# A transformer layer with routed experts: expert rows in units of 256 slots, outputs scattered back by row number

## The chip, the cores and the metric

The kernel runs on one core of a Trainium2 chip. The metric is the time of one launch on the device, in microseconds (us), as the median of several runs. The profile comes from one further execution, whose own time is given beside its span.

## The reference

One layer: a normalised input goes through causal attention with 16 heads and through a mixture of experts, and both are added to the input. 16 batches of 256 tokens give 4096 tokens of 128 numbers.

```python
xn = layernorm(x)
x  = x + attention(xn) + moe(xn)

def moe(x):                                   # 4096 tokens, H = 128, F = 512, E = 8, TOP_K = 2
    probs = softmax(x @ Wg)
    vals, idx = top_k(probs, 2)
    weights = vals / (sum(vals) + 1e-9)       # two weights for each token
    y = silu(x @ W1[e] + b1[e]) @ W2[e] + b2[e]        # for the token's two experts
    shared = silu(x @ Ws1 + bs1) @ Ws2 + bs2
    return sum_over_two(weights * y) + 0.1 * shared
```

## The kernel before

The first two thirds of the launch are attention: 64 groups of four heads run through a software pipeline whose beats `(t, s)` are written out in one loop for each engine. The router works beside it, on groups of 8 tiles (1024 tokens). For each token and each of its two experts it finds a place in a table of rows in HBM, `rows_d` (`expert_rows`), in which each expert has a region of its own. POOL writes the normalised rows there by indirect DMAs of 128 rows each (`scatter`, L851), one or two in a beat. Near the end of attention `list_blocks` on DVE turns the counts into a list of blocks: a block is 512 slots of one expert. SP fills the unused slots of an expert's last block with zeros (`fill`).

After attention come the passes (`PASSES`, `NP` = 31). A pass takes 512 tokens through two layers. A shared pass, of which there are 8 (two first, six last), reads its tokens in order from a store of split, turned rows. A routed pass (23, `NB`) loads the 512 rows of one block and the two weight matrices of its expert, both by a number read from the block list. 23 is the number that is enough for every possible distribution of 8192 rows over 8 experts in whole blocks of 512.

Each operand is in two parts (a high part and the rest), and each product takes three matmuls. In iteration `m` of the final loop PE issues: `turn_block(m+2)` (4 transposes, L1843), `hidden(m+1)` (12 matmuls of 512 columns, L1861), `expert_out(m)` (8 at L1952 and 4 at L1956), and `turn_out(m-1)` (4 transposes, L1967). A shared pass has no `turn_block`. ACT applies bias and silu (L1094), makes two of the high parts (L1100), adds the second bias (L1106) and copies the turned rows (L1075). DVE makes the low parts (L1586), the other high parts (L1584), the low part of the rows (L1573) and reads the turned output (`read_out`: L1595 into `yb` for a routed pass, L1600 into the residual `xres` for a shared one).

SP stores `yb` to `outs_d` (`expert_outs`), in the order of slots (`store_y`). When enough blocks are done, POOL gathers for each tile of tokens and each of the two picks 128 rows by number (L903, 64 indirect DMAs, at places `out_at`), four groups of 16, each group only when the blocks that may hold its rows are stored. DVE multiplies each by its weight and adds it to `xres` (`add_experts`, L1611, four operations of 128 columns for a chunk and a pick), at the iterations in `ADD_AT`. SP stores a chunk of the output when it is complete (`store_chunk`, L740).

SP issues all its DMAs in program order, and waits in that order too: at each iteration `after_turn`, `after_hidden`, `after_out`, `store_y`, `store_chunk`. Before the passes it issues the loads of the first two blocks.

## Time and profile before

| | |
|---|---|
| median of 3 runs | 688.34 us (686.59 to 688.4) |
| the profiled execution, its own time | 686.96 us |
| its span | 685.2 us |
| PE busy | 640.0 us, 93% |
| DVE, ACT, POOL busy | 77%, 77%, 62% |
| mean granted PE clock | 0.99 of full speed |

Busy shares are means over stages with different limits. The span falls into attention (to about 462 us), a passage of some 20 us, and the passes (from about 483 us to the end). Times in the views are us from the start of the span.

### The profile page before, as it was taken

Reading aid. Unit: us, or ns where it says so; the run is one execution under the profiler, and the core shown is the slowest. Engines: PE = TensorE matmul, PEld = TensorE weight load, DVE = VectorE, ACT = ScalarE, POOL = GpSimd, SP = SyncE. Lnnn points to the kernel's source line nnn. Section 1 sums busy time; section 2 is a strip of 40 time slices with the busy share of each in tenths; the row PEclk is TensorE's granted clock in tenths of the full one; section 3 lists DMA queues with packets and bytes.
Section 4 is the critical chain, followed back from the end, with each engine's and each line's share of the span. In section 5 each row is a group of like instructions: output and inputs, shape, how many; then the busy total and the mean of one; then the engine's idle time right before and its main releaser. Section 6 shows DMA issues by size and latency. Waiting matters only on the chain.

```text
span 685.2 us, 16441 instructions
## 1 busy us (share of the span) xinstructions
PE 640.0 (93%) x5478; PEld 550.1 (80%) x5478; DVE 527.4 (77%) x1338; ACT 527.2 (77%) x1070; POOL 425.4 (62%) x435
## 2 busy tenths in 40 slices
PE   4789999899999999999999999987999999999994
PEld 3778888788888888888888888875788888888883
DVE  7677787777778876768777788765879977788895
ACT  3678888888888888888788888873877777777772
POOL 4878776797887888878787675850000001755783
PEclk9999999999999999999999999998999999999998
DMA  6303213032132130202120100334458777888653
GB/s 174 114 3 109 72 41 111 27 100 87 38 122 67 58 117 10 93 30 64 61 68 14 35 13 19 95 123 152 156 193 247 238 245 240 299 274 275 212 148 88
DMA packets 51969, 79.37 MB, mean 116 GB/s; under 512 B 6305, under 2 KB 31886, under 8 KB 51886
## 3 DMA queue, kind: packets, MB, share of 16 engines
q1 hardware_dynamic: 47358, 69.82, 31.8%
q0 software_dynamic: 4096, 8.40, 4.4%
q8 instruction: 45, 0.74, 0.5%
q14 instruction: 38, 0.31, 0.1%
q10 hardware_dynamic: 432, 0.10, 0.1%
HBM read 47.82 MB, written 29.88 MB: 113 GB/s over the span
## 4 chain that ended last, share of the span: by engine, by line
PE 62%; DVE 12%; POOL 11%; ACT 6%; issue 6%; DMA 1%; POOLq 0%; DVEq 0%; ACTq 0%; SPq 0%
PE bank L1691 7%; PE bank L1952 7%; PE projections L1861 5%; PE bank L1861 5%; PE bank L1742 4%; PE bank L1728 4%; PE bank L1956 3%; POOL QK L903 3%; PE bank L1731 3%; PE bank L1706 3%; PE bank L1709 3%; PE projections L1675 2%; DVE mx L1248 2%; POOL heads_parted L794 2%; ACT QK L982 2%
## 5 line engine op out<-in xcount | busy, mean ns | idle before, releaser
L982 ACT ACTIVATE QK<-bank 120x512 fp32r<-120x512 f32 x256 | 155.0, 607 | 21.3 <-PE bank L1691 15.8
L976 ACT ACTIVATE prob<-bank 128x384 f32<-128x384 f32 x256 | 128.0, 501 | 52.9 <-PE bank L1731 52.9
L903 POOL DMA_INDIRECT QK<-expert_outs,out_at x64 | 67.4, 1053 | 149.4 <-DMA expert_outs<-prob 130.8
L1248 DVE TENSOR_REDUCE mx<-bank 128x3 f32<-128x384 f32 x256 | 140.9, 551 | 21.0 <-PE bank L1709 19.7
L1691 PE MATMUL bank<-identr,heads_parted 128*120 128x128 f32 x1024 | 135.6, 257 | 9.1 <-POOL heads_parted L794 5.4
L794 POOL TENSOR_TENSOR heads_parted<-rot,heads_parted 128x640 fp32r<-128x640 f32 x64 | 99.9, 1561 | 35.3 <-ACT heads_parted L1009 34.9
L1691 PEld LDWEIGHTS bank<-identr,heads_parted 128*120 128x120 f32 x1024 | 104.6, 139 | 15.8 <-POOL heads_parted L794 6.3
L1586 DVE TENSOR_TENSOR QK<-vaug,QK 128x512 fp32r<-128x512 f32 x124 | 86.1, 697 | 28.8 <-ACT QK L1100 25.7
L789 POOL TENSOR_TENSOR rot<-rot,t 128x512 f32<-128x512 f32 x64 | 82.2, 1284 | 24.2 <-DVE t L1241 24.0
L1706 PE MATMUL bank<-QK 120*128 120x256 f32 x256 | 93.1, 364 | 3.2 <-DVE mx L1248 2.3
L1728 PE MATMUL bank<-QK 122*128 122x256 f32 x256 | 89.5, 350 | 3.2 <-DMA QK<-mT 3.0
L1009 ACT ACTIVATE heads_parted<-rot 128x1280 fp32r<-128x1280 f32 x64 | 82.3, 1286 | 2.1 <-POOL rot L789 2.0
L851 POOL DMA_INDIRECT expert_rows<-xn,place_of x64 | 65.0, 1016 | 21.4 <-issue 10.9
L1233 DVE TENSOR_TENSOR rot<-projections,rope_table 128x640 f32<-128x640 f32 x64 | 52.5, 821 | 32.6 <-PE projections L1679 30.7
L1731 PE MATMUL bank<-identb,mask_qk 128*128 128x256 bf16 x256 | 73.3, 286 | 0.0
L1709 PE MATMUL bank<-mask_qk,identb 128*128 128x256 bf16 x256 | 73.0, 285 | 0.0
L1729 PE MATMUL bank<-QK 122*128 122x128 f32 x256 | 57.1, 223 | 0.0
L1707 PE MATMUL bank<-QK 120*128 120x128 f32 x256 | 57.0, 223 | 0.0
L1706 PEld LDWEIGHTS bank<-QK 120*128 120x128 f32 x256 | 51.5, 201 | 5.1 <-ACT QK L982 3.4
L1728 PEld LDWEIGHTS bank<-QK 122*128 122x128 f32 x256 | 48.8, 191 | 5.2 <-DMA QK<-mT 3.1
L1266 DVE TENSOR_TENSOR mT<-bank,mT 4x256 fp32r<-4x256 f32 x64 | 26.4, 412 | 30.2 <-ACT mT L990 29.8
L1707 PEld LDWEIGHTS bank<-QK 120*128 120x128 f32 x256 | 49.4, 193 | 0.0
(253 smaller groups left out, 1579.9 us busy)
## 6 DMA issues: line engine op xcount, KB each, us to landing
wb<-weight_parts SPq DMA_DIRECT2D x46, 512.0 KB, 4.8
weight_parts<-wb SPq DMA_DIRECT2D x18, 512.0 KB, 3.3
rot<-expert_rows SPq DMA_DIRECT2D x23, 256.0 KB, 4.3
expert_outs<-prob SPq DMA_DIRECT2D x23, 256.0 KB, 4.9
xn<-in_L_ffn_W SPq DMA_DIRECT2D x16, 256.0 KB, 3.8
xn_parts<-wb SPq DMA_DIRECT2D x16, 256.0 KB, 2.8
heads_parted<-xn_parts SPq DMA_DIRECT2D x8, 512.0 KB, 5.0
expert_rows<-zeros SPq DMA_DIRECT2D x15, 256.0 KB
```

What stands on the lines that cost most here:

```text
L794: nc.gpsimd.tensor_tensor(low_of(g), rotated(g), high_of(g)[:, :, 0:D], ALU.subtract).then_inc(s_lo, 1)
L903: nc.gpsimd.indirect_dma_start(out=gy[:, t, k, :], out_offset=None, in_=outs_d[0:READY[q] * SLOTS, :], in_offset=bass.IndirectOffsetOnAxis ...
L976: act_f(prob[:, g % 2 * HG + n, :], ST_PS[n % 2][:, 0:3 * P], ACT.Exp, scale=SCALE).then_inc(s_exp, 1)
L982: act_f(stacked(g, i), B_PS[bank_of(k)][0:KQ, :].rearrange("p (h t) -> p h t", h=HG), ACT.Copy)\
L1248: V.tensor_reduce(mx[:, g % 2, 0:3, n], B_PS[bank_of(k)][:, 0:3 * P].rearrange("p (a c) -> p a c", a=3), AX.X, ALU.max, negate=True).then_ ...
L1586: V.tensor_tensor(aparts[:, m % 2, 1, c, :], act[c], high, ALU.subtract).then_inc(s_alo, 1)
L1691: ins = nc.tensor.transpose(B_PS[bank_of(k)][0:KQ, n * P:(n + 1) * P].bitcast(F32R), parted(g)[:, j * PH + 2 * n + odd, :], identr[:, :])
L1706: mm(ps[:, 0:T], q[:, P:T], kk, start=True, stop=False, skip_group_check=True)
L1707: mm(ps[:, T:3 * P], q[:, 0:P], kk[:, 0:P], start=False, stop=False, skip_group_check=True)
L1709: mm(diag, identb[:, :], mask_qk[:, :].unsqueeze(1).to_broadcast([P, 2, P]), start=False, stop=True, skip_group_check=True).then_inc(s_bfi ...
L1728: mm(ps[:, P:3 * P], k[:, 0:P], q, start=True, stop=False, skip_group_check=True)
L1731: mm(diag, mask_qk[:, :], identb[:, :].unsqueeze(1).to_broadcast([P, 2, P]), start=False, stop=True, skip_group_check=True).then_inc(s_st, 1)
```

## The change

The unit of an expert's region becomes 256 slots. An expert's full units go in pairs through "d" passes (one expert, 512 slots), and what is left over, at most one unit for each expert, goes in pairs through "h" passes, in which 256 columns belong to one expert and 256 to another. 16 d passes and 4 h passes are enough for every distribution, 20 routed passes in place of 23, in the order h, d, h, d, h, d, h, d, then 12 d. With the shared ones `NP` is 28. The list has 24 entries (a d pass has one, an h pass two), each with its own weights: 8 of the 24 weight loads belong to h passes. Six sets of weights are held, in place of two, and all six are loaded ahead of the first routed pass.

In an h pass each matmul of 512 columns becomes two of 256 with different weights, and each of ACT's operations with a bias becomes two.

A row in `rows_d` gets four more numbers: the row number 2 * token + pick, the weight of that pick, and two zeros. DVE writes both for pick 0 (`V.tensor_copy` to columns C and C+1 of `xn`); a group of tiles scatters its 8 first picks, then POOL waits until these have landed, writes number and weight of pick 1 (`tag_second`), and scatters the other 8. An unused slot has a row number that is too large.

A loaded block so carries its own places and weights. DVE takes them (`out_row`, `out_wgt`), multiplies each output row by its weight as it reads it from PSUM, and POOL scatters the 4 x 128 rows of a pass straight to `outs_d` in the order of tokens (`scatter_out`). A too large number is changed to a spare row. When all 20 passes have landed, at iteration 24, SP loads `outs_d` in eight contiguous DMAs of 512 KB, one for a chunk of four tiles, and DVE adds each chunk and pick in one operation of 512 columns, all at iterations 24 to 27. The whole second half of `list_blocks`, which worked out where to gather, is gone.

```diff
-PASSES = [("s", 0), ("s", 1)] + [("r", i) for i in range(NB)] + [("s", c) for c in range(2, CHUNKS)]
+UNIT = SLOTS // 2
+DOUBLES = 2 * TILES * P // SLOTS
+SINGLES = E
+ROUTED = [step for i in range(SINGLES // 2) for step in (("h", i), ("d", i))] + \
+    [("d", i) for i in range(SINGLES // 2, DOUBLES)]
+PASSES = [("s", 0), ("s", 1)] + ROUTED + [("s", c) for c in range(2, CHUNKS)]
+W_SETS = 6
+RW = C + 4
-ADD_AT = {18: ((0, 0),), 19: ((0, 1),), 20: ((1, 0),), 21: ((1, 1),), 22: ((2, 0),), 23: ((2, 1),), 24: ((3, 0),),
-          25: ((3, 1), (4, 0)), 26: ((4, 1),), 27: ((5, 0), (5, 1)), 28: ((6, 0),), 29: ((6, 1),), 30: ((7, 0), (7, 1))}
-STORE_AT = {20: 0, 22: 1, 27: 2, 28: 3, 29: 4, 30: 5}
+ADD_AT = {24: ((0, 0), (0, 1)), 25: ((1, 0), (1, 1), (2, 0)), 26: ((2, 1), (3, 0), (3, 1), (4, 0)),
+          27: ((4, 1), (5, 0), (5, 1), (6, 0), (6, 1), (7, 0), (7, 1))}
+STORE_AT = {25: 0, 26: 1, 27: 2}
+LOAD_AT = 24
...
+            sp.wait_ge(s_st, HG * PER * (B - 1))
+            load_rows(0)
+            for part in range(2):
+                for entry in range(2):
+                    load_weights(entry, part)
+            load_rows(1)
+            for entry in range(2, W_SETS):
                 for part in range(2):
-                    load_weights(r_, part)
+                    load_weights(entry, part)
...
             def after_turn(m):
                 if is_routed(m):
-                    sp.wait_ge(s_xt, PASSES[m][1] + 1)
-                    load_rows(PASSES[m][1] + 2)
+                    sp.wait_ge(s_xt, routed_no(m) + 1)
+                    sp.wait_ge(s_own, 2 * (routed_no(m) + 1))
+                    load_rows(routed_no(m) + 2)
...
+            def load_outs():
+                for n in range(2):
+                    sp.wait_ge(s_yst[n], 16 * 4 * (NR // 2))
+                for c in range(CHUNKS):
+                    first = 4 * c * P
+                    sp.dma_start(gy[:, 4 * c:4 * c + 4, :, :],
+                                 outs_d[2 * first:2 * (first + SLOTS), :].rearrange("(t p k) c -> p t k c", p=P, k=2))\
+                        .then_inc(s_g[c], 16)
...
+            def tag_second(q):
+                ts = slice(q * GT, (q + 1) * GT)
+                pool.wait_ge(s_sc[q], 16 * GT)
+                nc.gpsimd.tensor_scalar(xn[:, ts, C], row_no[:, ts], 1.0, None, ALU.add).then_inc(s_tag2, 1)
+                nc.gpsimd.tensor_copy(xn[:, ts, C + 1], wgt[:, ts, 1]).then_inc(s_tag2, 1)
+                pool.wait_ge(s_tag2, 2 * (q + 1))
...
+            def scatter_out(r):
+                pool.wait_ge(s_own, 2 * (r + 1))
+                pool.wait_ge(s_ye, PASSES.index(ROUTED[r]) + 1)
+                for i in range(4):
+                    nc.gpsimd.indirect_dma_start(
+                        out=outs_d, out_offset=bass.IndirectOffsetOnAxis(ap=out_row[:, r % 4, i:i + 1], axis=0),
+                        in_=yb[r % 2][:, i, :], in_offset=None).then_inc(s_yst[r % 2], 16)
...
-                    act_f(act[c], banks[c][:, :], ACT.Silu, bias=bias_of(m, c)).then_inc(s_act[c], 1)
+                    for cols, its_bias in biases_of(m, c):
+                        ins = act_f(act[c][:, cols], banks[c][:, cols], ACT.Silu, bias=its_bias)
+                    ins.then_inc(s_act[c], 1)
...
+                if r_ >= 4:
+                    dve.wait_ge(s_ye, PASSES.index(ROUTED[r_ - 4]) + 1)
+                    dve.wait_ge(s_yst[r_ % 2], 16 * 4 * (r_ // 2 - 1))
+                V.tensor_tensor(out_row[:, r_ % 4, :], xb[r_ % 2][:, :, C], spare_row[:, r_, :], ALU.min).then_inc(s_own, 1)
+                V.tensor_copy(out_wgt[:, r_ % 4, :], xb[r_ % 2][:, :, C + 1]).then_inc(s_own, 1)
...
-                    V.tensor_copy(yb[i % 2], turned).then_inc(s_ye, 1)
+                    V.tensor_tensor(yb[r_ % 2], turned, out_wgt[:, r_ % 4, :].unsqueeze(2).to_broadcast([P, 4, C]), ALU.mult)\
+                        .then_inc(s_ye, 1)
...
-                for t in range(4 * c, 4 * c + 4):
-                    ins = V.scalar_tensor_tensor(out=xres[:, t, :], in0=gy[:, t, k, :], scalar=wgt[:, t, k:k + 1],
-                                                 in1=xres[:, t, :], op0=ALU.mult, op1=ALU.add)
+                chunk = xres[:, 4 * c:4 * c + 4, :]
+                V.tensor_tensor(chunk, gy[:, 4 * c:4 * c + 4, k, :], chunk, ALU.add).then_inc((c_g, s_fin)[k], 1)
...
                 for c in chunks:
                     at_least(pe, s_act[c], m)
-                    for i, (part, a) in enumerate(((0, 0), (0, 1), (1, 0))):
-                        ins = mm(banks[c][:, :], w[:, part * F + c * P:part * F + (c + 1) * P], xT[m % 2][:, a, :],
-                                 start=(i == 0), stop=(i == 2))
+                    for w, cols in its:
+                        for i, (part, a) in enumerate(((0, 0), (0, 1), (1, 0))):
+                            ins = mm(banks[c][:, cols], w[:, part * F + c * P:part * F + (c + 1) * P], xT[m % 2][:, a, cols],
+                                     start=(i == 0 and cols.start == 0), stop=(i == 2), skip_group_check=True)
```

The parts of the activation (`aparts`) and the loaded outputs (`gy`) have exchanged their halves of `QK`; the fills are halved in size and six fewer; and two of the router's small parts stand one to six beats earlier.

## Rows read from the trace of the kernel before

**Rows 1.** The page: busy time and share of each engine.
```profile
PE 640.0 (93%) x5478; PEld 550.1 (80%) x5478; DVE 527.4 (77%) x1338; ACT 527.2 (77%) x1070; POOL 425.4 (62%) x435
```

**Rows 2.** Busy time by stretch: attention, routed passes, shared passes at the end.
```profile
300.00:400.00 100.00, 96.25 (x1019) 84.92 (x1017) 76.93 (x216) 84.06 (x182) 76.05 (x75) 1.00 0.15 47
...
600.00:620.00 20.00, 20.00 (x100) 16.42 (x99) 16.66 (x37) 15.16 (x26) 11.96 (x12) 1.00 0.89 277
640.00:660.00 20.00, 20.00 (x95) 16.44 (x94) 18.23 (x41) 13.85 (x23) 15.58 (x15) 1.00 0.57 164
```

**Rows 3.** Timeline of PE, one iteration of a routed pass: start, us, what.
```profile
507.55 0.60 PE L1843 MATMUL bank<-ident,rot 128*128 128x128 f32 x4
507.91 1.65 PE L1861 MATMUL projections<-heads_parted,wb 128*128 128x512 f32 x6
...
510.79 2.03 PE L1952 MATMUL bank<-QK,wb 128*128 128x512 f32 x8
...
513.59 0.60 PE L1967 MATMUL bank<-ident,prob 128*128 128x128 f32 x4
514.02 0.60 PE L1843 MATMUL bank<-ident,rot 128*128 128x128 f32 x4
```

**Rows 4.** Timeline of PE, the last three iterations (shared passes).
```profile
660.25 1.64 PE L1861 MATMUL projections<-heads_parted 128*128 128x512 f32 x6
...
666.17 1.64 PE L1861 MATMUL projections<-heads_parted 128*128 128x512 f32 x6
...
672.10 2.09 PE L1952 MATMUL bank<-QK,heads_parted 128*128 128x512 f32 x8
...
676.41 0.63 PE L1967 MATMUL bank<-ident,prob 128*128 128x128 f32 x4 [0.87 <-DVE xres L1600]
```

**Rows 5.** Timeline of DVE near the end.
```profile
655.33 0.68 DVE L1600 TENSOR_TENSOR xres<-bank,xres 128x512 f32<-128x512 f32 x1
655.93 1.12 DVE L1611 SCALAR_TENSOR_TENSOR xres<-QK,wgt,xres 128x128 f32<-128x128 f32 x4
...
677.38 2.31 DVE L1611 SCALAR_TENSOR_TENSOR xres<-QK,wgt,xres 128x128 f32<-128x128 f32 x8 [1.12 <-DMA QK<-expert_outs,out_at]
679.80 0.69 DVE L1600 TENSOR_TENSOR xres<-bank,xres 128x512 f32<-128x512 f32 x1
```

**Rows 6.** Groups of ACT by shape: silu of 512 columns, copy of 256 columns.
```profile
L1094 ACT ACTIVATE vaug<-projections,xn 128x512 f32<-128x512 f32 x46 | 31.7, 690 | 2.8 <-PE projections L1861 0.5
...
L1062 ACT ACTIVATE heads_out<-bank 128x256 f32<-128x256 f32 x31 | 11.8, 379 | 0.0
```

**Rows 7.** The gathers of L903: ns min/median/max with first and last start; landing; group.
```profile
L903 POOL DMA_INDIRECT QK<-expert_outs,out_at x64: 940/947/2284, 579.3 to 674.8; - x64
...
DMA to landing us min/median/max: 2.5/4.1/6.3
...
L903 POOL DMA_INDIRECT QK<-expert_outs,out_at x64 | 67.4, 1053 | 149.4 <-DMA expert_outs<-prob 130.8 <-issue 17.1 <-PE bank L1861 1.3
```

**Rows 8.** Timeline of SP: the first loads for the routed passes.
```profile
474.63 0.36 SPq L659 DMA_DIRECT2D rot<-expert_rows  x1
475.77 1.47 SPq L667 DMA_DIRECT2D wb<-weight_parts  x2
```

**Rows 9.** One microsecond of these loads: the last two columns are DMA share and GB/s.
```profile
480.00:481.00 1.00, 0.94 (x5) 0.53 (x4) 0.34 (x2) 0.99 (x4) 0.00 (x0) 1.00 1.00 395
```

**Rows 10.** Timeline of PE: the third routed block's rows are turned.
```profile
494.60 0.60 PE L1843 MATMUL bank<-ident,rot 128*128 128x128 f32 x4
```

**Rows 11.** Timeline of POOL in attention, at one pair of row scatters.
```profile
382.95 0.98 POOL L851 DMA_INDIRECT expert_rows<-xn,place_of  x1
384.24 0.96 POOL L851 DMA_INDIRECT expert_rows<-xn,place_of  x1 [0.30 <-issue]
...
386.10 1.55 POOL L794 TENSOR_TENSOR heads_parted<-rot,heads_parted 128x640 fp32r<-128x640 f32 x1 [0.90 <-ACT heads_parted L1009]
```

More of the change, by code:

```diff
@@ L217, in scatters_at @@
     if 61 <= t < 67:
[L218 removed]
+        first = (0, 3, 6, 8, 11, 14, 2 * GT)[t - 61:t - 59]
+        return GROUPS - 1, tuple(range(*first))
     return None, ()
@@ L494, in build @@
         s_ye = sem("expert_out_read")
-        s_yst = [sem(f"expert_out{n}_stored") for n in range(2)]
-        s_g = [sem(f"chunk{n}_gathered") for n in range(CHUNKS)]
+        s_yst = [sem(f"expert_out{n}_scattered") for n in range(2)]
+        s_g = [sem(f"chunk{n}_loaded") for n in range(CHUNKS)]
         c_g = sem("dve_first_experts_added")
@@ L1359, in router @@
                     if q == GROUPS - 1:
-                        steps.add(V.tensor_tensor(count[:, :], found[:, q, :], ebase[:, :], ALU.add))
+                        steps.add(V.tensor_tensor(count[:, :], found, ebase[:, :], ALU.add))
                         steps.need()
@@ L1374, in take @@
                         t.rearrange("p (a c d) -> p a c d", c=shape[1], d=shape[2])
-                upto = take(GROUPS + 1, E)
-                size, start, end, first = (take(GROUPS, E) for _ in range(4))
-                before_q, shift, code, no, row = take(GROUPS), take(SEGS + 1), take(NB), take(NB), take(NB)
+                halves, before_e = take(2, E), take(2, E)
+                ends, shift, odd_at = take(SEGS), take(SEGS + 1), take(E)
                 coded, leap = take(SEGS + 1), take(SEGS)
-                moved, place, turned, step, limit = take(2 * TILES), take(2 * TILES), take(SEGS), take(SEGS), take(SEGS)
-                chosen, second = take(NB, E), take(NB, E)
+                code, no, row, chosen, second = take(NE_IN), take(NE_IN), take(NE_IN), take(NE_IN, E), take(NE_IN, E)
                 at = used[0]
-                deep = take(GROUPS, E, E)
+                over, deep = take(E, 2 * E), take(2, E, E)
                 used[0] = at
-                sel, bound = take(NB, SEGS), take(NB, E - 1)
+                sel, bound = take(NE_IN, SEGS), take(NE_IN, E - 1)
                 used[0] = at
-                passed = take(2 * TILES, SEGS)
-                used[0] = at
-                parts = take(NB, FC, E)
-                flat2 = lambda t: t.rearrange("p a c -> p (a c)")
-                by_block = lambda t, w: t.unsqueeze(2).to_broadcast([P, NB, w])
-                each = lambda t, w: t.unsqueeze(1).to_broadcast([P, NB, w])
-                by_q = lambda t: t.unsqueeze(1).to_broadcast([P, GROUPS, E])
+                parts = take(NE_IN, FC, E)
+                by_entry = lambda t, w: t.unsqueeze(2).to_broadcast([P, NE_IN, w])
+                each = lambda t, w: t.unsqueeze(1).to_broadcast([P, NE_IN, w])
+                doubled = 2 * DOUBLES
                 steps.need()
@@ L1418, in list_blocks @@
                 steps.need()
[L1419 to L1420 removed]
+                steps.add(V.tensor_tensor(ends[:, E + 1:SEGS], odd_at, halves[:, 0, :], ALU.add))
+                steps.add(V.scalar_tensor_tensor(out=odd_at, in0=odd_at, scalar=-float(UNIT), in1=ebase[:, :], op0=ALU.mult,
+                                                 op1=ALU.add))
                 steps.need()
[L1422 to L1423 removed]
+                steps.add(V.scalar_tensor_tensor(out=shift[:, E + 1:SEGS], in0=halves[:, 1, :], scalar=float(SLOTS), in1=odd_at,
+                                                 op0=ALU.mult, op1=ALU.add))
@@ L1430, in list_blocks @@
                 yield
-                steps.add(V.tensor_tensor(sel, by_block(block_no, SEGS), each(flat2(end), SEGS), ALU.is_ge))
+                steps.add(V.tensor_tensor(sel, by_entry(unit_at[:, :], SEGS), each(ends, SEGS), ALU.is_ge))
                 steps.need()
```

375 lines of the change are left out of this document (186 added, 189 removed).

## The prediction, made before the changed kernel was run

> **What bounds the kernel now.** I read the page's busy times first, then the stages, then PE's own timeline in the passes, then the ends of the other engines. PE is busy 93% of the span and no other engine's compute is above 77% [rows 1]. By stages the reader should see two things [rows 2]: in attention PE is busy 96.25 of 100 us with POOL and ACT at 76 and 84, so it is PE with small holes that the others cause; in the passes PE is busy 20.00 of 20.00 us at full clock, while DVE has 1.8 to 3.3 us to spare in 20 and DMA moves 277 GB/s at a share of 0.89. In the passes the time is therefore the number of PE instructions times their pace, and nothing that DVE, ACT, POOL or the DMAs give back there counts, unless it stands at the end.
>
> One routed iteration lasts from one `turn_block` to the next: 514.02 - 507.55 = 6.47 us [rows 3]. Inside it `hidden` takes 510.79 - 507.91 = 2.88 by starts, which is its 12 matmuls at about 0.233 (2.80) and a start-up, `expert_out` the same, and each set of four transposes some 0.43. A shared iteration has no `turn_block` and lasts 666.17 - 660.25 = 5.92 us [rows 4].
>
> At the end PE is not last. Its last transposes start at 676.41 [rows 4], but DVE adds the last gathered chunk from 677.38, reads the last pass at 679.80 and is done at 680.5 [rows 5]; stores and the end bring this to 685.2.
>
> **The change, part by part.** The sum is made against the profiled execution: 686.96 us, of which 685.2 is span; it is 1.4 below the median of 688.34.
>
> 1. *Three routed iterations fewer.* 3 x 6.47 = 19.4 us off PE's stream [rows 3]. The count is in the program, whatever the data. The passes are PE-bound on both sides of these, so the whole amount counts. -19.4.
>
> 2. *Halved matmuls in the four h passes.* 24 matmuls of 512 columns become 48 of 256. Per matmul the row shows 0.233 us where 512 columns at full clock (2.4 GHz) are 0.213, so some 0.020 is for the instruction. Then 24 more instructions cost 24 x 0.020 = 0.48 us a pass, 1.9 for four. From the other side, the transposes take 0.43 / 4 = 0.108 us for 128 columns (0.053), so 0.055 is the dearest price of an instruction that this trace shows for a new set of weights: 24 x 0.055 x 4 = 5.3. From below it is 0, if columns alone count. The 0.020 is from the very matmuls that are halved, so I take +1.9, bounds 0 and +5.3.
>
> 3. *ACT in an h pass.* Four silus and a bias of 512 columns (0.69 each) become ten of 256; a copy of 256 is 0.38 [rows 6]. 5 x (0.76 - 0.69) = +0.35 us on ACT. From the stage's row ACT is busy 15.16 of 20 us [rows 2], 4.9 a pass; with 5.3 of now 6.95 it stays hidden under PE. 0.
>
> 4. *DVE in a pass.* Two operations on four columns, under 0.2 us each, and the weight comes into the operation that already reads PSUM. 16.66 of 20 us [rows 2] is 5.4 a pass, and this contains adds that are now elsewhere. Hidden, 0. The places of the gathers are no longer worked out, which was hidden too.
>
> 5. *POOL scatters each pass.* The nearest rows are the gathers: 1.053 us each on average, with 0.30 between two [rows 7], so four take 5.4 us of 6.47. They begin after `read_out`, and what waits for them is the `read_out` two passes later (`yb` has two buffers), 12.9 us on. The last is issued some 4.1 us after the first and lands 4.1 us later in the median, 6.3 at most [rows 7]: 8.2 to 10.4 us. It fits, with 2.5 us to spare in the worst case. Hidden, 0; if that cover is gone each further microsecond counts 20 times (the second rival).
>
>    The 64 gathers ran beside the same copies and casts of DVE (two casts and one or two copies a pass) and took 1.053 us in the mean and 2.284 at most [rows 7]. The Trainium skill, page "SBUF — State Buffer", section "SBUF: two separate sides", speaks against this change: while DVE runs an fp32 copy in its two-port mode, GpSimd cannot write the descriptors of its own DMAs; a section below ("A bandwidth-pool intuition that's wrong") gives 3.1 us for such a transfer that takes 0.62 alone. By that figure, as an estimate, four would take 12.4 us and bound each of 20 passes, +119; by the rows nothing is added.
>
> 6. *The first loads.* SP now issues 15 DMAs before the loop, not 6, at 1.14 us each [rows 8]: from about 474 to 490. The rows for the third routed pass (`load_rows(2)`, two DMAs) come behind these in SP's queue, so at 491 to 492, and behind 6.8 MB in the rings. At the 395 GB/s of [rows 9] these take 17 us, to 491.5; at the 277 GB/s of [rows 2] 24.6, to 499. PE wants those rows at 494.6 [rows 10], or 0.2 later, since half of the first h pass stands before. So a wait of 0 to 4 us, once. Since SP's issuing paces it rather than the rings, I take +0.5. All weights needed earlier are ahead of these in the queue.
>
> 7. *Attention.* POOL now waits in each group for its first eight scatters. With one a beat the eighth has long landed; only in the third group do the eighth and the ninth stand in one beat. There the first of the pair is issued at 382.95 and the second at 384.24 [rows 11]. With the gathers' least time of 2.5 us to landing the second must wait to 385.5, then two small operations, and ends near 387.1, where `take_low` began at 386.10. Behind it on POOL stand `take_low` and the rotation's add, and PE's transposes of the heads wait for these: +1.0 at most once. Tags, constants and the moved router steps add some 20 short DVE and POOL operations of 0.1 to 0.2 us over 460 us; PE's holes there are 4% [rows 2] and take part of them. I take +0.7, bounds 0 and +3. The halved fills and the shorter list relieve DMA and DVE, neither of which bounds; 0.
>
> 8. *The end.* I write it in the old clock, with PE's last four iterations starting at 654.3, 660.25, 666.17 and 672.1. The last routed output is turned in iteration 22, which starts five shared iterations before the last one, at 642.5; DVE reads such an output 6.9 us after its iteration starts (655.33 [rows 5], in the one from 648.4), so it is done at 650.1. Its four scatters start at 1.35 us intervals, the last at 654.2, and that lands 4.1 us later, at 658.3. SP reaches the loads at the end of `hidden(25)`, 654.3 + 2.9 = 657.2, puts a chunk load first, and so starts them near 658.3 by either cause. 4.2 MB at 277 GB/s are 15 us and the landing 2, so they arrive from 662 to 675, one every 1.9 us. DVE's adds are operations of 512 columns, at 0.60 from start to start [rows 5]. Two in iteration 24, three in 25, four in 26: 2.4 us there where 1.1 stood, so `read_out(26)` comes at 676.1 and not at 675.58. In the last iteration seven adds, 4.2 us, stand between it and `read_out(27)`: 676.7 + 4.2 = 680.9, done at 681.7, where 680.5 was. +1.2. If the loads go no faster than the 164 GB/s of [rows 2], they end at 658.3 + 25.6 + 2 = 685.9; one pair of adds and the read bring 687.8: +7. From below, the adds cannot begin earlier: 0. The eight output stores were already in the tail, and the last has the same place after `read_out`.
>
> Sum: -19.4 + 1.9 + 0.5 + 0.7 + 1.2 = -15.1, so 686.96 - 15.1 = 671.9 in the profile's terms. The runs' median stood 1.4 above; I put the forecast halfway, 672.5 us.
>
> **The rivals.**
>
> *Likeliest, 0.64:* as summed. With the nearer ends of the bounds its own range is 668 to 676.
>
> *The end waits for its loads, 0.12.* All 4.2 MB now start in the last 28 us, where the gathers had from 579 to 675 [rows 7]. For it: DVE has nothing to do but wait, and SP issues them only after the last scatter has landed. Against it: the rows show 277 GB/s at mixed sizes. +2 to +6 beyond my sum: 674 to 679.
>
> *The scatters set the pace of the routed passes, 0.07; slower than before.* The place is DVE's `read_out` waiting for `yb`. One scatter longer than 6.47 / 4 - 0.30 = 1.32 us in the mean makes POOL the bound; 15.1 us are lost when a pass takes 6.47 + 0.75 = 7.2 us, at 1.5 us a scatter. If each took the 2.28 us of the longest gather [rows 7], 20 passes of 10.3 us would give +77, about 750 us. For it: a gather can take 2.28. Against it: the mean of 64 beside the same casts and copies of DVE is 1.053. This is the case that the page named in step 5 describes.
>
> *Halves and first loads cost their upper bounds, 0.12.* +3.4 and +3.5 over the sum: 676 to 680.
>
> *It gains nothing, 0.02:* 688. The count of passes is fixed in the program, so this would need a new wait of 0.75 us in each pass. The last 0.03 is for a gain above 22 us, if the holes of attention close with fewer fills.
>
> **How the numbers follow.** A time within 0.3% (2 us) cannot be told from no change. Faster: 0.64 + 0.12 + 0.12 + 0.03 = 0.91; same 0.02; slower 0.07. The range has to leave out no more than 2 in 10: it takes the likeliest case, the late loads and most of the dear halves, 667 to 680.
>
> **What would show it.** Right: a d iteration of 6.47 us and an h iteration of 6.9 to 7.0 on PE, PE at 20.00 of 20 in the passes; no DVE wait on the scatter of outputs; the eight loads starting just after the last scatter lands, 28 us before the end, and DVE's last seven adds in a row. Wrong: a DVE or PE wait in every second iteration, released by an output scatter; PE idle before the third `turn_block`, with a lower granted clock behind it; gaps between the last adds, each released by a load. The forecast fails most likely if the last DMAs or POOL's issuing are slower than their nearest rows.

## The result, and the profile after

The changed kernel takes 766.25 us in the median (764.6 to 766.89) where the kernel before takes 687.84 in the same comparison: a ratio of 1.114 (95% interval 1.111 to 1.116). Forecast were 672.5 us and a gain. Its profiled span is 762.8 us, 77.6 more than the 685.2 of before. PE has the same number of matmuls and is busier in us, but idle far more. First the page's busy time and share, to be read against [rows 1]:

```profile
PE 657.8 (86%) x5478; PEld 558.9 (73%) x5478; DVE 505.8 (66%) x1313; ACT 515.3 (68%) x1066; POOL 438.6 (57%) x463
```

Then busy time by stretch, beside [rows 2]. Attention has lost 1.6 us in 100; in the passes every engine stands still for part of the time, PE from 20.00 down to 15.53, DVE to 7.40. The granted clock, the third column from the right, is below 1.00 there.

```profile
300.00:400.00 100.00, 94.66 (x995) 83.27 (x993) 76.18 (x210) 83.18 (x183) 75.74 (x78) 1.00 0.10 31
600.00:620.00 20.00, 15.53 (x62) 11.69 (x60) 7.40 (x18) 7.48 (x13) 7.67 (x8) 0.84 0.44 145
640.00:660.00 20.00, 14.78 (x56) 11.24 (x57) 9.39 (x20) 9.54 (x16) 6.64 (x7) 0.83 0.48 152
```

When no engine is busy, the waits say what they have in common. The view of waits (total us, times, longest):

```profile
POOL expert_outs L957 <- DVE prob L1642: 159.5, 17, 54.4
DVE out_row L1618 <- DMA expert_outs<-prob,out_row: 104.4, 16, 8.7
ACT vaug L1151 <- DVE QK L1632: 77.2, 17, 8.3
...
PE bank L2002 <- DVE QK L1630: 44.7, 25, 6.1
```

(The 54.4 in the first row is one wait, POOL's for the first routed output.) It is a ring: PE waits for DVE's low parts, ACT for DVE, POOL for DVE's `read_out` (L1642), and DVE, in front of an operation of 0.16 us (L1618, the row numbers into `out_row`), for POOL's scatters to land. One turn of it on DVE, and the scatters on POOL:

```profile
600.01 0.68 DVE L1642 TENSOR_TENSOR prob<-bank,out_wgt 128x512 f32<-128x512 f32 x1
600.61 0.68 DVE L1614 TENSOR_TENSOR heads_parted<-bank,heads_parted 128x512 fp32r<-128x512 f32 x1
607.56 0.16 DVE L1618 TENSOR_TENSOR out_row<-rot,spare_row 128x4 uint32<-128x4 f32 x1 [6.27 <-DMA expert_outs<-prob,out_row]
...
607.71 1.29 DVE L1632 TENSOR_TENSOR QK<-vaug,QK 128x512 fp32r<-128x512 f32 x2
...
611.04 0.68 DVE L1642 TENSOR_TENSOR prob<-bank,out_wgt 128x512 f32<-128x512 f32 x1
...
618.59 0.16 DVE L1618 TENSOR_TENSOR out_row<-rot,spare_row 128x4 uint32<-128x4 f32 x1 [6.26 <-DMA expert_outs<-prob,out_row]
```

```profile
601.45 0.96 POOL L957 DMA_INDIRECT expert_outs<-prob,out_row  x1 [6.47 <-DVE prob L1642]
602.71 0.96 POOL L957 DMA_INDIRECT expert_outs<-prob,out_row  x1 [0.30 <-issue]
...
605.24 0.96 POOL L957 DMA_INDIRECT expert_outs<-prob,out_row  x1 [0.30 <-issue]
612.48 0.95 POOL L957 DMA_INDIRECT expert_outs<-prob,out_row  x1 [6.29 <-DVE prob L1642]
```

The reader should see that a pass now lasts from one `read_out` to the next, 611.04 - 600.01 = 11.03 us, where 6.47 stood in [rows 3]; and that no scatter is slower than forecast: four are issued 1.26 us apart and the last, issued at 605.24, has landed by 607.56. DVE simply asks for them at once. `out_row` and `out_wgt` have four slots. In iteration m `block_low(m + 2)` writes the slot that pass m - 2 used, and the `read_out` of pass m - 2 is what DVE has just done, at the end of iteration m - 1. So the whole trip of the scatters, from 600.69 to 607.56, lies bare in each of 16 passes, with DVE's low parts for the next `expert_out` queued behind it. On PE it shows in the second product of the same pass:

```profile
606.14 1.07 PE L2002 MATMUL bank<-QK 128*128 128x512 f32 x4
609.39 0.84 PE L2002 MATMUL bank<-QK 128*128 128x512 f32 x2 [2.18 <-DVE QK L1630]
```

Two smaller losses stand ahead of the passes. The first routed block is turned 14.06 us later (497.44; before 483.38). And the third one's rows come late, as against the row without a wait in [rows 10]; behind the wait a projection of 6 matmuls takes 2.80 us, 1.7 times its 1.65 of [rows 3], while the granted clock is 0.57 (from 514 to 518 us), near the lower of its two levels:

```profile
513.75 0.66 PE L1884 MATMUL bank<-ident,rot 128*128 128x128 f32 x4 [4.54 <-DMA rot<-expert_rows]
514.16 2.80 PE L1906 MATMUL projections<-heads_parted,QK 128*128 128x512 f32 x6
```

The end, beside [rows 4] and [rows 5], went nearly as forecast: the last seven adds of DVE are in a row, its last `read_out` follows, and PE's last transposes wait for DVE.

```profile
751.45 2.61 DVE L1660 TENSOR_TENSOR xres<-QK,xres 128x512 f32<-128x512 f32 x4
...
754.58 4.67 DVE L1660 TENSOR_TENSOR xres<-QK,xres 128x512 f32<-128x512 f32 x7
759.36 0.69 DVE L1649 TENSOR_TENSOR xres<-bank,xres 128x512 f32<-128x512 f32 x1
```

From PE's last iteration (748.27) to the end of the span are 14.5 us; before it was 685.2 - 672.10 = 13.1.

### The profile page after: what moved, and what is told of

Read it like the earlier page. It is cut to its first block, busy times and chain, and to the rows that moved or that the text cites. A ratio compares the mean times of both kernels' runs of the same rounds, so it can differ in the third digit from the quotient of the medians.

```text
span 762.8 us, 16452 instructions
## 1 busy us (share of the span) xinstructions
PE 657.8 (86%) x5478; PEld 558.9 (73%) x5478; DVE 505.8 (66%) x1313; ACT 515.3 (68%) x1066; POOL 438.6 (57%) x463
## 4 chain that ended last, share of the span: by engine, by line
PE 37%; DVE 20%; issue 13%; POOL 13%; DMA 8%; ACT 6%; SPq 2%; DVEq 0%; POOLq 0%; ACTq 0%
POOL expert_outs L957 8%; PE bank L1733 6%; DMA expert_outs<-prob,out_row 6%; PE bank L1784 4%; PE bank L1770 3%; DVE QK L1632 3%; PE bank L1748 2%; DVE mx L1316 2%; PE bank L1773 2%; PE bank L1751 2%; PE projections L1717 2%; DVE QK L1630 2%; DVE rot L1301 2%; ACT QK L1039 2%; DVE prob L1642 2%
## 5 line engine op out<-in xcount | busy, mean ns | idle before, releaser
L957 POOL DMA_INDIRECT expert_outs<-prob,out_row x80 | 78.0, 975 | 178.7 <-DVE prob L1642 159.5
L1733 PE MATMUL bank<-identr,heads_parted 128*120 128x128 f32 x1024 | 136.5, 259 | 15.1 <-POOL heads_parted L844 7.2
L1632 DVE TENSOR_TENSOR QK<-vaug,QK 128x512 fp32r<-128x512 f32 x112 | 75.6, 690 | 12.9 <-ACT QK L1158 10.7
L1151 ACT ACTIVATE vaug<-projections,xn 128x512 f32<-128x512 f32 (+1 forms) x48 | 27.1, 617 | 78.5 <-DVE QK L1632 76.8
L1618 DVE TENSOR_TENSOR out_row<-rot,spare_row 128x4 uint32<-128x4 f32 x20 | 3.2, 161 | 104.4 <-DMA expert_outs<-prob,out_row 104.4
L2002 PE MATMUL bank<-QK 128*128 128x512 f32 (+1 forms) x128 | 38.0, 418 | 32.0 <-DVE QK L1630 32.0
L1748 PEld LDWEIGHTS bank<-QK 120*128 120x128 f32 x256 | 52.3, 204 | 7.6 <-DVE mT L1334 3.7
```

The source lines that it names most:

```text
L957: nc.gpsimd.indirect_dma_start(out=outs_d, out_offset=bass.IndirectOffsetOnAxis(ap=out_row[:, r % 4, i:i + 1], axis=0), in_=yb[r % 2][:, i ...
L1632: V.tensor_tensor(aparts[:, m % 2, 1, c, :], act[c], high, ALU.subtract).then_inc(s_alo, 1)
L1733: ins = nc.tensor.transpose(B_PS[bank_of(k)][0:KQ, n * P:(n + 1) * P].bitcast(F32R), parted(g)[:, j * PH + 2 * n + odd, :], identr[:, :])
L1748: mm(ps[:, 0:T], q[:, P:T], kk, start=True, stop=False, skip_group_check=True)
```

## The experiments

Theory A is the ring above. B says that the scatters themselves cost the passes their pace. C and D are two causes of attention's delay: the two last router parts in earlier beats, or the tag work. E is about the first loads. Where a time is set against another kernel's, both ran on chips on which the kernel before took 686.5 to 687.8 us. The exceptions are the runs with six slots, with later adds, with places and loads once more, and without the weights: their chips ran the kernel before in 704 to 707 us.

### A slot for each pass

`out_wgt` alike, and every `% 4` on the two goes:

```diff
-        out_row = sb("out_row", [P, 4, 4], U32)
+        out_row = sb("out_row", [P, NR, 4], U32)
...
-                if r_ >= 4:
-                    dve.wait_ge(s_ye, PASSES.index(ROUTED[r_ - 4]) + 1)
-                    dve.wait_ge(s_yst[r_ % 2], 16 * 4 * (r_ // 2 - 1))
```

> The changed kernel with 20 slots for the places and weights taken from a block, one for each routed pass, in place of 4; DVE then has no slot to wait for. Theory A: the wait for the slot is the whole loss of the passes. In the trace of the changed kernel an iteration of a routed pass lasts 11.03 us (from the scatter at 601.45 to that at 612.48) where PE needs 6.47, and DVE waits 104 us in 16 times. From the first turned block to the last iteration the changed kernel takes 250.8 us; without the wait it should take 188.7 - 19.4 as the kernel before less three iterations, and some 6 for the wait on the first rows: 175. So 766 - 75 = 691 us, between 687 and 696, and no DVE wait released by an output scatter. Theory B: the scatters are too slow in themselves, and the wait moves to the reading of the output two passes later: above 715 us.

690.15 us, 1.006 of the kernel before (1.004 to 1.009): of 766.25, 76 us are gone by giving 20 passes 20 slots. In its trace the operation that waited has no idle time before it (group row: busy, mean ns, idle), PE is full at full clock, and the scatters are not even shorter (1.061 us each in the mean, 0.975 in the changed kernel):

```profile
L1615 DVE TENSOR_TENSOR out_row<-rot,spare_row 128x4 uint32<-128x4 f32 x20 | 3.0, 148 | 0.0
```

```profile
540.00:640.00 100.00, 100.00 (x534) 84.90 (x533) 75.13 (x153) 76.22 (x130) 66.97 (x63) 1.00 0.68 224
```

Theory A is shown and B falls: the wait on the four slots is what the passes lost. What remains, 690 in place of 672.5, is elsewhere.

### Five slots, and six

The same wait, for the pass five (or six) back:

```diff
-                if r_ >= 4:
-                    dve.wait_ge(s_ye, PASSES.index(ROUTED[r_ - 4]) + 1)
-                    dve.wait_ge(s_yst[r_ % 2], 16 * 4 * (r_ // 2 - 1))
+                if r_ >= 5:
+                    dve.wait_ge(s_ye, PASSES.index(ROUTED[r_ - 5]) + 1)
+                    dve.wait_ge(s_yst[(r_ - 5) % 2], 16 * 4 * ((r_ - 5) // 2 + 1))
```

> The changed kernel (766.25 us) with five slots in out_row and out_wgt in place of four; the wait ahead of the tags stays, for the pass five back. Theory A (the tags of pass m+2 waited for scatters whose rows DVE had finished one instruction earlier): the scatters waited for are now a whole pass of 6.5 us older, and four scatters issued 1.26 us apart plus 2.3 us of landing, 7.4 us after their read_out, are just about done: 690.5 us (689 to 694), as with a slot for each pass. Rival: the chip can't take four scatters in a pass of 6.5 us, so they fall behind whatever the slots: over 705.

698.44 us, which is neither. The group's idle time is down from 104.4 us in 16 waits to 33.3 in 10, and the timeline tells why some is left:

```profile
L1618 DVE TENSOR_TENSOR out_row<-rot,spare_row 128x4 uint32<-128x4 f32 x20 | 3.2, 158 | 33.3 <-DMA expert_outs<-prob,out_row 33.3
```

```profile
559.80 0.68 DVE L1642 TENSOR_TENSOR prob<-bank,out_wgt 128x512 f32<-128x512 f32 x1
...
561.00 0.15 DVE L1618 TENSOR_TENSOR out_row<-rot,spare_row 128x4 uint32<-128x4 f32 x1
...
564.79 0.68 DVE L1642 TENSOR_TENSOR prob<-bank,out_wgt 128x512 f32<-128x512 f32 x1
...
571.50 0.16 DVE L1618 TENSOR_TENSOR out_row<-rot,spare_row 128x4 uint32<-128x4 f32 x1 [5.43 <-DMA expert_outs<-prob,out_row]
```

The scatters of the `read_out` at 559.80 are waited for from 566.07 on. They needed until 571.50, for POOL issued the last of them at 566.01 and from there to 571.5 the DMA share is 1.00 (400 GB/s). I had given them 7.4 us and got 11.7; and the bare slack of the fifth slot is one iteration, less DVE's work up to the wait. The passes then go in pairs, one short and one long.

> Six slots for the tags. With five (698.44 us) a scatter still had to land 5.3 us after its read_out began to be waited for (559.80 to 566.07) and landed 11.6 us after it. Theory A, with that slack worked out rightly: a sixth slot adds one iteration of 6.4 us to the 5.3, 11.7 us, which covers it: no or almost no wait left, 690.5 us (689 to 692). Rival: the scatters of one pass delay those of the next more and more, so that no number of slots short of one per pass is enough: 693 to 697.

```profile
L1618 DVE TENSOR_TENSOR out_row<-rot,spare_row 128x4 uint32<-128x4 f32 x20 | 3.0, 152 | 0.0
```

No wait is left: idle time before it is 104.4, 33.3, 0.0 us with four, five and six slots. The time, 699.72 us, can't be held against the 690.15: the chip of this comparison ran the kernel before in 706.8 us (700.15 to 716.23). By ratio it is 0.992 of that (0.989 to 0.996), where a slot per pass had 1.006; but the kernel of places and loads (below) also has a ratio lower by 0.010 on such a chip, so the time decides nothing here and the idle time does. On this chip DVE waits 7.5 us in 8 times ahead of `read_out`, which it never does with a slot for each pass on the first one: 1.2 us for scatters to land, 3.7 with a releaser that the trace doesn't name.

### The tags later in DVE's order

Four slots, but the tags of pass m + 2 are taken behind `activation_low(m + 1)`:

```diff
                 activation_low(m + 1)
+                take_tags(m + 2)
                 if m:
                     read_out(m - 1)
```

> The changed kernel with its 4 slots, but DVE takes places and weights after the low parts of the activation and not before them. Theory A (what costs is where the wait stands in DVE's order, right behind the reading of the very pass whose scatter it waits for): the 3.9 us of low parts now cover part of the 6.3 us from that reading to the landing; the cycle is 6.3 + 0.2 + 0.6 = 7.1 us in place of 11.03, about 10 us over the 6.47 of the run with a slot for each pass: 699 to 707 us. If only the number of slots counted and the wait were the same wherever it stands: about 766. Theory B (slow scatters): as now, above 740.

748.27 us, a miss: only 18 of 76 us came back. DVE still waits 76.1 us at that place, and PE has a new wait:

```profile
DVE out_row L1624 <- DMA expert_outs<-prob,out_row: 76.1, 16, 7.6
...
PE bank L1891 <- DMA rot<-expert_rows: 33.2, 15, 5.1
```

I had left out who waits for the tags: SP's `load_rows` of the next block may overwrite `xb` only when they are taken (`s_own`), so it went out at 608.96, a microsecond after the tags, and PE waited for rows. The `read_out` behind the tags is late too, and with it the next scatters. A wait with a full round trip in it isn't mended by a place 3 us later. The time is one that I had given to theory B (above 740), but the 20 slots had ruled B out already, and the scatters take 0.96 us in the median here as there.

### The moved router parts, in the kernel before

```diff
-SPREAD = ((8, 3), (10, 3), (11, 3), (12, 3), (13, 3), (14, 2), (14, 3), (16, 3), (17, 3), (18, 3))
-DENSE = ((8, 3), (9, 3), (10, 0), (10, 3), (11, 0), (11, 2), (11, 3), (12, 3), (13, 0), (13, 3))
+SPREAD = ((8, 3), (10, 3), (11, 3), (12, 3), (13, 3), (14, 2), (14, 3), (16, 3), (15, 2), (15, 3))
+DENSE = ((8, 3), (9, 3), (10, 0), (10, 3), (11, 0), (11, 2), (11, 3), (12, 3), (12, 0), (12, 1))
```

> The kernel before, with only the two last parts of the router moved to the beats that they have in the changed kernel. In the changed kernel attention ends 14 us later. Theory C: the moved parts are most of it, since POOL's trace is later by 2.0 us at the 15th beat, by 2.2 at the 31st, by 1.5 near the 47th and by some 6 near the 60th, where these parts now stand: 696 to 700 us. Theory D: the row tags, POOL's wait for the first eight scatters and the fuller scatters are the cause, and the moved parts are hidden: 687 to 690.

695.59 us, +9.1 for the kernel before by two router parts in other beats (ratio 1.014, 1.012 to 1.015). The last low part of attention on POOL is a good clock for this; each row gives ns (min, median, max) and first and last start, of before, after and this kernel:

```profile
L794 POOL TENSOR_TENSOR heads_parted<-rot,heads_parted x64: 1535/1557/1746, 17.4 to 450.3; 128x640 fp32r<-128x640 f32 x64
```

```profile
L844 POOL TENSOR_TENSOR heads_parted<-rot,heads_parted x64: 1533/1552/1732, 17.3 to 463.4; 128x640 fp32r<-128x640 f32 x64
```

```profile
L794 POOL TENSOR_TENSOR heads_parted<-rot,heads_parted x64: 1538/1559/1749, 17.4 to 459.3; 128x640 fp32r<-128x640 f32 x64
```

So the places by themselves make 9.0 us of delay, where the changed kernel has 13.1. The other 4.1 come in one step: at the low part before the last the two kernels are late alike, 8.9 and 9.0 us (table below). What happens at the moved parts shows in the changed kernel, in the last group of tiles. DVE, then POOL:

```profile
427.99 1.10 DVE L1406 TENSOR_TENSOR rsm<-two 128x8 f32<-128x8 f32 x1
429.13 0.82 DVE L1301 TENSOR_TENSOR rot<-projections,rope_table 128x640 f32<-128x640 f32 x1
...
431.83 1.04 DVE L1413 TENSOR_TENSOR wgt<-two,rsm 128x16 f32<-128x16 f32 x1
```

```profile
427.52 1.55 POOL L844 TENSOR_TENSOR heads_parted<-rot,heads_parted 128x640 fp32r<-128x640 f32 x1 [1.57 <-ACT heads_parted L1066]
431.56 1.28 POOL L839 TENSOR_TENSOR rot<-rot,t 128x512 f32<-128x512 f32 x1 [2.49 <-DVE t L1309]
```

An operation on 8 columns takes 1.10 us and ends at 429.09, just behind the 429.07 at which POOL's operation ends; the other ends at 432.87 and POOL's at 432.84. The same operation took 0.17 in the kernel before (L1338). These operations stand in front of the rotation and the maxima, which PE waits for: from 420 to 440 PE is busy 16.53 us at a clock of 0.83, before 18.92 at 1.00. The Trainium skill, page "SBUF — State Buffer", section "SBUF: two separate sides", has the rule: a VectorE operation with two inputs in SBUF and a GpSimd operation that reads SBUF exclude each other for a whole instruction. These rows agree: the short one ends 0.02 to 0.03 us behind POOL's.

The stretch alone is not the price, though. Four operations of the two parts are at times longer than at others (L1334, L1338, L1341, L1345 of the kernel before, once for each group of tiles). They take 4.7 us in all in the kernel before and 8.7 with the parts moved: 4.0 us more, against a delay of 9.0. What stands behind them in DVE's queue must count as well; how the 9.0 are shared out is not shown.

### Slots and places together

The slot per pass, and parts 8 and 9 at (15, 0), (16, 2) and (12, 1), (12, 2).

> The run with a slot for each pass, and the two router parts in other beats: one beat step (15,0) and one (16,2), where DVE of the kernel before stands idle for 1.1 us each, and for the last group (60,1) and (60,2). Theory C: 4 to 8 us faster than with the slots alone. Theory D: no more than 1 us faster.

685.52 us, 4.6 less than with the slots alone, as theory C has it; the last low part starts at 457.8 in place of 462.8. Yet the same four operations take 10.3 us here and not 8.8: two of them, on 8 columns, now take 1.02 and 1.09 us in the mean. A longer stretch at a place where less waits behind it cost less.

### The first loads

```diff
             load_rows(1)
-            for entry in range(2, W_SETS):
+            for entry in range(2, W_SETS - 2):
...
                     load_rows(routed_no(m) + 2)
+                    if routed_no(m) == 0:
+                        for entry in range(W_SETS - 2, W_SETS):
+                            for part in range(2):
+                                load_weights(entry, part)
```

> The kernel with a slot per pass (690.15 us), and of its first loads the sets 4 and 5 (2 MB, four DMAs) are issued behind the third block of rows, not ahead of it. Theory E: the third block's rows come late only because of what was issued ahead of them (PE waited 4.54 us for them at 513.75 in the changed kernel and then ran at half clock); with a third of it gone the wait goes, and some of the half clock: 684.5 us (683 to 687). Rival: the rows come late because of their own descriptors, or the two sets are then late themselves in the third routed pass: 689 to 692.

> The same edit of the first loads on the kernel with a slot per pass and two router parts placed elsewhere (685.52 us, its PE waited 4.39 us for the rows): by theory E 680 us (678 to 682), which would be below the kernel before (686.46). By the rival 685 to 687.

684.79 and 679.61 us: 5.4 and 5.9 less than without the edit, both as theory E forecast. The second is 0.990 of the kernel before (0.987 to 0.992), 7 us faster, and the best version of this study. Its fourth block is now the one that is late, by little:

```profile
511.60 0.66 PE L1885 MATMUL bank<-ident,rot 128*128 128x128 f32 x4 [1.41 <-DMA rot<-expert_rows]
```

### The end

On POOL, behind its last scatter:

```diff
+            for m in sorted(ADD_AT):
+                for c, k in ADD_AT[m]:
+                    if k == 0:
+                        pool.wait_ge(s_g[c], 16)
...
+                        nc.gpsimd.tensor_tensor(chunk, gy[:, 4 * c:4 * c + 4, 0, :], chunk, ALU.add).then_inc(c_g, 1)
```

> The kernel of the run before with places and loads mended (expected at 680), and at the end the eight adds of the first expert (k = 0) are on POOL, which has nothing else then; DVE keeps the eight of the second. Eight adds of 0.69 us leave DVE, 5.5 us, but DVE waited 2.6 us for the loads among them, and POOL's add takes nearer 1.3 us, which shows behind the last load: 678 us (676 to 680). Rival: POOL's adds and DVE's slow each other, or the last load sets the end alone: 680 to 682.

688.07 us, 8.5 more than without it and outside both forecasts. An add that takes DVE 0.69 us takes POOL 1.6, and the last ones stand in a chain with DVE's reads of the shared passes, which they wait for:

```profile
671.26 1.57 POOL L974 TENSOR_TENSOR xres<-QK,xres 128x512 f32<-128x512 f32 x1 [4.02 <-DVE xres L1658]
674.12 3.24 POOL L974 TENSOR_TENSOR xres<-QK,xres 128x512 f32<-128x512 f32 x2 [1.29 <-DVE xres L1658]
```

The other try moved adds to later iterations: the first chunk's two from 24 to 25, and one from 25 to 26. It was run twice, the second time with the kernel of places and loads beside it.

> The kernel of places and loads (679.61 us) with the first chunk's two adds moved from iteration 24 to 25 and one add from 25's third place to 26's first is unchanged otherwise, so that 25 has four adds. DVE waited 3.28 us for the first load at 655.44 and from there ran back to back to the end; with the low parts ahead of that wait they fill it: 677.5 us (676.5 to 679). Rival: the last iterations are then as full, and the end hangs on the loads and the eight adds of the last chunks alone: 679 to 680.5.

> The later adds once more. In its trace the tail from the read_out before the first add to DVE's end took 20.91 us against 23.67 with places and loads alone: 2.8 us less than the run beside it (2 to 3.3), 676.8 us where that takes 679.6. Rival: the 2.8 us were lost again earlier (DVE waited 4.18 us at 650.20 in it): 0 to 1 us less.

> The kernel of places and loads once more, so that the next two stand beside it on one chip: in the last three comparisons the kernel before took 706.8 us where it had taken 686.5, so they can't be set against 679.61. By its ratio 0.9895 it should take 1.0 to 1.1% less than the kernel before on a chip where that takes 686.5.

685.74 us; then 690.07 against 689.92 for places and loads, with spreads of 8.1 and 6.2 us, on a chip that ran the kernel before in 704.34. The wait for the first loads is gone from DVE's row, but no gain can be told; in the run beside it DVE waited just 0.70 us there, not 3.28. That fits the rival of the second forecast: DVE's waits ahead of `read_out` are 15.5 us in this trace and 6.8 in the one beside it (none at all in the run of 679.61 us), nearly all without a named releaser. Whether they are the scatters of the pass two back is not shown. Inconclusive. Nor did the ratio carry over: places and loads took 0.980 of the kernel before on this chip (0.974 to 0.985), not 0.990, so the kernel before loses more on such a chip than the changed one.

### What is left in attention

Six of the eight short operations of parts 8 and 9 are left out, four times each (DVE has 1289 instructions and not 1313); the two that fill the tag columns stay.

> The kernel of places and loads (679.61 us) with the eight short DVE operations left out that work out the two experts' weights for each group of tiles (parts 8 and 9 of the router); the tag columns get the row numbers in their place, so the outputs are not weighted. All waits of the tags stay. Theory C: what is left of the attention's delay (its last low part on POOL begins at 458.2 against 450.3 before) is mostly these parts standing ahead of the maxima that POOL and PE wait for: about 5 us go, 674.5 us (672 to 677). Rival D': it is the tag work on POOL and its wait for the first scatters: 678 to 680.

> The kernel of places and loads without the eight short DVE operations of router parts 8 and 9, once more. Theory C: 3 to 5 us less than the run of places and loads beside it (on the other chip it was 1.8 us below the later adds, which are worth 2.2 to 2.8): 675.5 us where that takes 679.6. Rival D': under 1.5 us less.

683.91 us with no kernel of places and loads beside it; then 682.35 against 689.92, 7.6 less, more than either forecast. Spreads of 9.1 and 6.2 us make the 7.6 rough. The starts of POOL's low parts tell where it comes from. Us behind the kernel before (whose trace is from another chip in the last two rows):

| low part, of 64 | 15th | 31st | 47th | 60th | 61st | 63rd | 64th |
|---|---|---|---|---|---|---|---|
| changed kernel | 0.3 | 2.6 | 5.2 | 6.6 | 10.2 | 8.9 | 13.1 |
| kernel before, parts moved | 0.0 | 1.8 | 3.7 | 5.1 | 8.6 | 9.0 | 9.0 |
| slots and places | 0.1 | 1.3 | 3.1 | 3.9 | 5.5 | 3.4 | 7.5 |
| places and loads, once more | 0.3 | 1.6 | 3.8 | 4.6 | 6.3 | 6.5 | 10.9 |
| the same without the six operations | 0.1 | -0.2 | 1.0 | 0.7 | 1.1 | 0.3 | 4.7 |

Without the six operations the delay is all but gone up to the 63rd low part. But the kernel before computes them too, in its own beats, so this bounds their price and doesn't say how much a better place could give back. The last step, 4.1 to 4.4 us between the last two low parts, is in every kernel of the new form, with these operations or without, and not in the kernel before with its parts moved. There POOL waits for PE's beat, does the tags of the second picks, and issues three scatters ahead of its low part (changed kernel):

```profile
459.10 0.25 POOL L896 TENSOR_SCALAR xn<-row_no 128x8 f32<-128x8 f32 x1 [1.98 <-PE bank L1773]
...
459.78 1.07 POOL L913 DMA_INDIRECT expert_rows<-xn,place_of  x1 [0.28 <-POOL xn L897]
...
463.41 1.54 POOL L844 TENSOR_TENSOR heads_parted<-rot,heads_parted 128x640 fp32r<-128x640 f32 x1
```

So theory C holds for the delay up to there, and rival D' stays open for the last step, which falls where its tag work stands; whether the tags, the constants or the block list on DVE cause it, no run tests.

## Why the prediction was wrong

**The step that failed is 4**, with the half of step 5 that belongs to it. Step 4 costs the tags on DVE as "two operations on four columns, under 0.2 us each", hidden. They are (161 ns in the mean). But a wait stands ahead of them, and it wasn't priced. Step 5 worked out the trip of the scatters, 8.2 to 10.4 us, and set it against the wrong customer: "what waits for them is the `read_out` two passes later". That holds for `yb` with its two buffers; the tags' four slots are asked for sooner, since the tags are taken two passes ahead. When DVE takes those of pass m + 2, three slots are held by the passes m + 1, m and m - 1, whose `read_out` is still to come, and the fourth is that of pass m - 2, whose `read_out` DVE has just done. The cost is then arithmetic: `read_out` 0.68 us, from its end to the end of the wait 6.87, from there to the next `read_out` 3.48, together 11.03 in place of 6.47; 4.6 us in each of 16 passes are 73 us, and the 20 slots gave back 76. Six slots end the wait, as the runs show. The trip itself was mis-sized too: with five slots it took 11.7 us where the forecast's worst case was 10.4, so the two buffers of `yb` cover it with about 1 us to spare and not 2.5.

**The rival on the other side had the sign and the wrong place.** It wanted DVE's `read_out` to wait for `yb` and scatters of 1.5 us or more. They took 0.975 us in the mean, and `read_out` waited for `yb` 0.7 us in all; on the two slower chips, where DVE does wait ahead of `read_out`, that place may have cost something, as told above. The 3.1 us that the Trainium skill gives for such a transfer beside DVE's copies (page "SBUF — State Buffer", section "A bandwidth-pool intuition that's wrong"), cited in step 5, was not seen: the trace of the changed kernel has 80 scatters of 78.0 us in all. DVE stands idle beside many of those, so the better test is the run with a slot for each pass, where it doesn't: 84.9 us for the 80, 1.48 at most.

Point by point, in spans:

- Step 1, three iterations fewer, -19.4: right. With the slots mended PE is busy 100.00 of 100 us in the passes.
- Step 2, halved matmuls, +1.9: too dear. In the kernel of places and loads `hidden` takes 2.92 to 2.95 us by starts with 24 matmuls of 256 columns and 2.83 to 2.89 with 12 of 512; `expert_out` takes 2.84 to 2.88 against 2.74 to 2.80. That is some 0.17 us for an h pass, +0.7 in all, or 0.007 for each extra instruction; the 0.020 that I took from 0.233 - 0.213 doesn't belong to the instruction. One `hidden` of each kind, from its start to that of `expert_out`:

```profile
497.40 1.68 PE L1907 MATMUL projections<-heads_parted,QK 128*128 128x256 f32 x12
...
500.35 2.00 PE L2003 MATMUL bank<-QK,heads_parted 128*128 128x512 f32 x8
...
503.89 1.63 PE L1907 MATMUL projections<-heads_parted,QK 128*128 128x512 f32 x6
...
506.72 2.08 PE L2003 MATMUL bank<-QK 128*128 128x256 f32 x16
```

- Step 3, ACT: right, hidden.
- Step 6, first loads, +0.5 (bounds 0 to 4): mis-sized. PE waited 4.54 us, and the matmuls behind ran at half clock for a while; the edit that removes it gave 5.4 to 5.9. I let SP's issuing pace the loads. SP was on time (it issued these rows at 505.64, where the forecast's 491.5 and the 14.06 us of attention are 505.6), but a backlog stood in the rings: from 500 to 510 DMA moved 414 GB/s at a share of 1.03, and the rows came 24.8 us after the first of the loads (488.92), as in my slower case, though at a mean of 332 GB/s from 490 to 514: 8.0 MB and not 6.8. And the price of a stall has the clock behind it.
- Step 7, attention, +0.7 (bounds 0 to +3): mis-sized by most of what remained, +13.4 with the slots mended. The operations of "0.1 to 0.2 us" were priced by their own work. In their new beats some take 1.0 to 1.1 us, and end with POOL's long operation there, and they stand in front of work that PE waits for: 9.0 with the parts moved alone. POOL's wait for the scatters in the third group, priced at +1.0, made its low part 1.1 us later in one beat, and the next beat had taken that back. The step of 4.1 us at the last low part has no term in the forecast.
- Step 8, the end, +1.2: +1.4 in the changed kernel, but there the passes ran slowly. With the slots mended it is +2.7 (688.1 - 672.26 = 15.8 us from PE's last iteration, 13.1 before), and DVE waits 3.6 us for the first load: within the bounds, and partly what the rival of the late loads said.

The kernel with a slot per pass can be added up exactly from its trace, by three stretches. To the first turned block: +13.4 (496.73). From there to PE's last iteration (672.26): 175.5 us where 188.7 stood, which is -19.4 + 6.2. The end: +2.7. Together +2.9 over 685.2, its span of 688.1. Of the 6.2, PE's wait for the third block's rows is 4.92 and the halved matmuls some 0.7; the rest is the lower clock behind the wait and what else changed there, which I can't separate. So with the slots mended the forecast of -15.1 misses by 18.0, of which attention is 12.7, the first loads and that rest 5.0 and the end 1.5, less 1.2 for the halved matmuls.

## What to carry to other kernels

For each buffer that a change adds, count slots from the instruction that *takes* the slot, not from the one that uses it, and find the last event that it waits for in program order on its own engine: if that was started by the instruction just before, the buffer has no depth at all, whatever its size. A four-column operation may hide a round trip. And a short operation that is moved is not priced by its duration in the old beat, but by what runs beside it in the new one (here POOL's long operation, which it ended with) and by what stands behind it in its own queue; the runs show that both change and that the sum was 9 us, not the share of each.

## What the runs showed of the hardware

Short DVE operations on SBUF took 1.0 to 1.1 us in place of 0.16 to 0.17, and where it was looked at ended with a POOL operation of 1.28 or 1.55 us. Changing a set of weights every 256 columns cost little more than every 512 (2.92 to 2.95 against 2.83 to 2.89 us for the same columns). An add of 128x512 took 1.6 us on POOL and 0.69 on DVE. Four scatters of 128 rows, issued 1.26 us apart, had landed 2.3 us after the last was issued where the DMA share of these microseconds was 0.16, and 5.5 us after it where that was 1.00. For ten microseconds the core's DMA moved 414 GB/s. On two chips the kernel before took 704 to 707 us where it took 686.5 on the others, so that absolute times of different comparisons say little at this size of effect.
